# A two-layer vision tower: tokens of slots ahead of expert 0's rows, attention's end merged with the FFN's entry, and loads behind the K and Q casts

## The reference

```
h = patches(x) @ W_proj.T + b                     # 576 tokens (16 images x 36), 192 wide
h = h + attention(layernorm(h))                   # 12 heads of 64, softmax over the image's 36 tokens
h = h + ffn(layernorm(h))                         # BitLinear: rmsnorm, 8-bit activations, ternary weights
h = h + ttt_attention(layernorm(h))               # a state W1 per image and head, one gradient step
h = h + moe(layernorm(h))                         # 8 experts, the best 2 per token, capacity 180
```

## Time and profile before

| | |
|---|---|
| median of 3 runs | 268.79 us (268.14 to 273.12) |
| profiled execution, its own time | 268.12 us |
| its span, first to last instruction | 266.3 us |
| mean granted TensorE clock | 0.954 of 2.4 GHz |
| busy: PE, DVE, ACT, POOL | 229.8, 182.2, 160.1, 120.6 us |
| chain that ended last, by engine | PE 39%, DVE 26%, issue 11%, ACT 8%, POOL 8%, DMA 8% |

### The profile page before, as it was taken

The page is one execution under the profiler, slowest core; times in us unless marked ns, Lnnn a source line. Parts: engine busy times, 40 slices in busy tenths (PEclk is TensorE's granted clock), DMA queues, the critical chain, the costliest instruction groups (busy, mean ns, idle before and its releaser), DMA issues.

```text
span 266.3 us, 6234 instructions
## 1 busy us (share of the span) xinstructions
PE 229.8 (86%) x2368; PEld 176.0 (66%) x2368; DVE 182.2 (68%) x513; ACT 160.1 (60%) x302; POOL 120.6 (45%) x145
## 2 busy tenths in 40 slices
PE   8964899799489969988898999998999988999970
PEld 3741457587379956444496694975659778999960
DVE  1775367689998569779859879479875447455653
ACT  3623967878688970687589568384551384565300
POOL 9322199111323968564660005204304988845620
PEclk9999599999997988999999997999997999999996
DMA  6999785423290089990045005990660899842362
GB/s 192 296 275 187 116 197 138 99 61 69 61 219 16 2 148 203 205 202 11 0 39 72 0 2 50 137 138 4 68 132 28 135 158 176 110 77 29 33 149 72
DMA packets 25634, 28.66 MB, mean 108 GB/s; under 512 B 11624, under 2 KB 20897, under 8 KB 25509
## 3 DMA queue, kind: packets, MB, share of 16 engines
q0 software_dynamic: 7744, 15.43, 39.7%
q1 hardware_dynamic: 17861, 12.83, 17.2%
HBM read 36.74 MB, written 4.81 MB: 156 GB/s over the span
## 4 chain that ended last, share of the span: by engine, by line
PE 39%; DVE 26%; issue 11%; ACT 8%; POOL 8%; DMA 8%; DVEq 0%; SPq 0%; POOLq 0%; ACTq 0%
PE bank L656 6%; PE bank L568 5%; DMA arena<-x_scratch,arena 4%; PE bank L585 4%; PE bank L536 3%; DMA y_sum<-arena 3%; POOL arena L1922 3%; DVE st L968 3%; PE bank L523 2%; PE bank L746 2%; PE bank L904 2%; PE bank L915 2%; POOL y_sum L1913 2%; PE bank L723 2%; PE bank L764 2%
## 5 line engine op out<-in xcount | busy, mean ns | idle before, releaser
L656 PE MATMUL bank<-tri,idh 128*128 128x512 f16 x148 | 40.3, 395 | 0.0
L1913 POOL DMA_INDIRECT y_sum<-arena x12 | 18.0, 1500 | 9.3 <-DMA y_sum<-arena 4.9
L1922 POOL DMA_INDIRECT arena<-x_scratch,arena x14 | 13.9, 994 | 16.7 <-DVE arena L1448 12.8
L1841 POOL TENSOR_TENSOR arena<-arena,ri 128x432 f32<-128x432 f32 x8 | 7.3, 911 | 31.2 <-DVE ri L1089 31.2
L656 PEld LDWEIGHTS bank<-tri,idh 128*128 128x128 f16 x148 | 14.1, 101 | 10.9 <-issue 2.2
L1813 POOL TENSOR_TENSOR rs<-arg,mhalf 128x1 f32<-128x1 f32 (+1 forms) x20 | 11.9, 596 | 16.2 <-DVE arg L972 14.8
L585 PE MATMUL bank<-arena,arena_k 96*128 96x288 f16 (+2 forms) x144 | 18.5, 286 | 0.0
L1400 DVE TENSOR_TENSOR arena<-bank,arena 128x360 f32<-128x360 f32 x16 | 8.4, 532 | 13.6 <-PE bank L904 10.5
L585 PEld LDWEIGHTS bank<-arena,arena_k 96*128 96x128 f16 x144 | 13.8, 98 | 3.8 <-issue 0.3
L568 PE MATMUL bank<-arena_k,arena 96*128 96x384 f16 (+1 forms) x60 | 13.0, 389 | 3.6 <-issue 3.6
L447 POOL DMA_DIRECT2D arena_v<-in_w x4 | 3.2, 804 | 27.2 <-ACT arena_v L442 27.2
(11 more groups left out here) (292 smaller groups left out, 645.7 us busy)
## 6 DMA issues: line engine op xcount, KB each, us to landing
arena_k<-in_w POOLq DMA_DIRECT2D x8, 512.0 KB, 7.5
arena_v<-in_w POOLq DMA_DIRECT2D x8, 512.0 KB, 10.5
arena_v<-in_xT SPq DMA_DIRECT2D x6, 288.0 KB, 4.1
arena_v<-v_scratch SPq DMA_DIRECT2D x32, 54.0 KB
v_scratch<-arena SPq DMA_DIRECT2D x4, 384.0 KB, 3.7
arena_k<-in_w POOLq DMA_DIRECT2D x8, 192.0 KB, 9.0
arena_v<-in_w POOLq DMA_DIRECT2D x8, 192.0 KB, 11.4
arena_k<-in_wqkv POOLq DMA_DIRECT2D x4, 288.0 KB, 9.9
```

The source lines that it names most:

```text
L656: mm(bank[IDLE][:, :], idh[:, :], tri[:, 0:1].broadcast_to([128, 512]), start=True, stop=True)
L1913: nc.gpsimd.indirect_dma_start(y_sum[k][:, :], bass.IndirectOffsetOnAxis(ap=sum_at[:, k, e:e + 1], axis=0), ys[:, e, D * k:D * k + D], Non ...
L1922: nc.gpsimd.indirect_dma_start(zr[:, e - 1, XW * k:XW * k + XW], None, x_scr[:, :], bass.IndirectOffsetOnAxis(ap=tok_at[:, k, e:e + 1], ax ...
```

## The change

It has three parts. (1) SP waits for K's and Q's casting loads before it issues the rows, the FFN's weights and the tables, and ACT negates K's high half after the first two transposed tiles and not before them. (2) The loop over pairs ends at `PAIRS`, and what its last four steps held is written out in one order with the FFN's entry, on PE, ACT and DVE; the product `wz` of the second attention comes into it, POOL prepares the second attention's rows before its softmax products, and the FFN's own steps are reordered, with fewer `keep_awake`. (3) In the mixture of experts the tokens of all slots are marked and multiplied before expert 0's rows are selected; `xsp` holds the last 64 columns twice, so that the selection takes 20 matmuls and not 30; loads of the experts' low halves move by one in POOL's list. The diff, cut to its core:

```diff
+TAIL_ORDER = [("PT", 5), ("wo", 0), ("wz", 0), ("PV", 4), ("PV", 5), ("PT", 6), ("wo", 1), ("PT", 7), ("wo", 2),
+              ("PV", 6), ("PV", 7)]
-        xsp = carve(at, 2, NT, D, dt=F16)
+        xsp = carve(at, 2, NT, XW, dt=F16)
+        ohc = stage_a[:, 0:NT * CAP].bitcast(F16).rearrange("p (x i n) -> p x i n", x=2, i=NT)
...
-        FFN_ORDER = [("xiT", 0), ("xiT", 1), ("xiT", 2), ("gate", 0), ("gate", 1), ("xiT", 3), ("xiT", 4)] + [
-            ("gate", i) for i in range(2, NT)]
+        FFN_ORDER = [("xiT", 0), ("xiT", 1), ("xiT", 2), ("gate", 0), ("gate", 1), ("gate", 2), ("xiT", 3), ("xiT", 4),
+                     ("gate", 3), ("gate", 4)]
+        DOWN_ORDER = [("yiT", 0), ("down", 0), ("yiT", 1), ("yiT", 2), ("down", 1), ("yiT", 3), ("down", 2), ("yiT", 4),
+                      ("down", 3), ("down", 4)]
...
@@ SP
             load(wqkvraw[:, :, WV_AT:], "wv", d["wqkv"][:, :, WV_AT:])
+            sp.wait_ge(loaded("wk"), 16)
+            sp.wait_ge(loaded("wq"), 16)
             load(rows[:, 0:o], "rows", d["rows"][0:o].partition_broadcast(128))
...
@@ PE
+            stages = {"PT": transposes, "wo": output_projection, "wz": state_kernels, "PV": values}
+            for key, n in TAIL_ORDER:
+                stages[key](n)
             pe.wait_ge(free[IDLE], idle_from)
             pe.wait_ge(loaded("tri"), 16)
-            keep_awake(8)
+            keep_awake(3)
+            for i in range(3, NT):
+                output_projection(i)
...
-                if (key, i) == ("xiT", 2):
-                    keep_awake(3)
...
-            for i in range(NT):
-                r = rows_of(i)
-                if i == 0:
-                    keep_awake(10)
...
                 fills(ins, "yiT", i)
-                keep_awake(2)
...
                 fills(ins, "down", i)
-                keep_awake(5 if i == 3 else 2)
...
+            keep_awake(4)
+            for key, i in DOWN_ORDER:
+                (yi_transposed if key == "yiT" else ffn_down)(i)
+                if key == "yiT":
+                    keep_awake(2)
+            keep_awake(4)
             for i in range(NT):
                 x_transposed("x1T", 1, (i,))
-                keep_awake(2)
+                keep_awake(1)
...
             fills(ins, "pos")
-            keep_awake(8)
+            keep_awake(15)
...
-                for out0, out1, c0, o in ((0, 128, 0, 0), (0, DT, 128, CAP), (DT, 128, 128, CAP)):
+                for j in range(2):
                     for x in range(2):
...
-                            ins = mm(bk[out0:out1, o:o + CAP], xsp[0:r, x, i, c0:c0 + out1 - out0],
+                            ins = mm(bk[:, CAP * j:CAP * j + CAP], xsp[0:r, x, i, 128 * j:128 * j + 128],
                                      oh[0:r, i, :], start=i == 0 and x == 0, stop=i == NT - 1 and x == 1)
...
+            tokens_of_slots()
             rows_selected(0)
-            keep_awake(1)
-            tokens_of_slots()
-            keep_awake(1)
+            keep_awake(6)
             for s in range(E + 1):
                 if s < E:
                     up_gate(s)
-                if s == 0:
-                    slot_weights()
                 if s + 1 < E:
                     rows_transposed(s + 1)
...
                 if s == 0:
-                    keep_awake(6)
+                    slot_weights()
+                    keep_awake(2)
...
@@ DVE
+            softmax_sums(7)
+            residual(0)
+            centred(0)
+            bk = wait_full(dve, "wz")
+            dve.wait_ge(rows_made, 1)
+            frees(v.tensor_copy(wb[:, :, D:2 * D], bk[0:HF, 0:2 * D].rearrange("p (c n) -> p c n", c=2)), "wz")
+            read_low(3)
+            softmax_low(6)
+            read_low(4)
+            softmax_low(7)
+            read_low(5)
+            for i in range(1, 3):
+                residual(i)
+                centred(i)
+            read_low(6)
+            read_low(7)
+            quantised(0, 3)
+            for i in range(3, NT):
+                residual(i)
+                centred(i)
+            gated(0)
+            quantised(3, NT)
+            gated(1)
+            gated(2)
+            y_largest(0)
...
+            choices()
             onehots(0)
             x_low(range(2, NT))
-            choices()
-            z_low(0)
+            dve.wait_ge(xs_hi, NT + 1)
+            for r, c in ((128, slice(0, NT - 1)), (rows_of(NT - 1), slice(NT - 1, NT))):
+                ins = v.tensor_tensor(xsp[0:r, 1, c, D:], xs[0:r, c, 128:], xsp[0:r, 0, c, D:], ALU.subtract)
+            ins.then_inc(xs_done, 1)
             token_index()
             routing_weights()
+            z_low(0)
...
@@ ACT
-            act.wait_ge(loaded("wk"), 16)
-            a(wqkv[:, 1, :, 768:1536], wqkv[:, 0, :, 768:1536], ACT.Copy, scale=-1.0).then_inc(wqk_negated, 1)
             for i in range(NT):
                 r = rows_of(i)
+                if i == 2:
+                    act.wait_ge(loaded("wk"), 16)
+                    a(wqkv[:, 1, :, 768:1536], wqkv[:, 0, :, 768:1536], ACT.Copy, scale=-1.0).then_inc(wqk_negated, 1)
                 bk = wait_full(act, "xnT", i)
...
+            transposes_copied(5, 0)
+            act.wait_ge(wq_sum, 2)
+            a(wiq[:], stage13[:], ACT.Identity, bias=nmagic[0:HF, 0:1]).then_inc(wq_done, 1)
+            transposes_copied(5, 1)
+            read_high(3)
+            softmax_high(6)
+            read_high(4)
+            softmax_high(7)
+            a(w2q[:], stage2[:], ACT.Identity, bias=nmagic[:, 0:1]).then_inc(wq_done, 1)
+            read_high(5)
+            transposes_copied(6, 0)
+            transposes_copied(6, 1)
+            act.wait_ge(loaded("wa"), 16)
+            a(wa16[:, 0], wa[:, :, :], ACT.Copy).then_inc(tw_hi, 1)
+            transposes_copied(7, 0)
+            transposes_copied(7, 1)
+            read_high(6)
+            read_high(7)
+            wait_evac(act, "wz")
+            act.wait_ge(loaded("lrT"), 16)
+            act.wait_ge(rows_made, 1)
+            a(wb16[:, 0], wb[:, :, :], ACT.Copy).then_inc(tw_hi, 1)
             table(ACT.Silu)
...
+            for r, c in ((128, slice(0, NT - 1)), (rows_of(NT - 1), slice(NT - 1, NT))):
+                ins = a(xsp[0:r, 0, c, D:], xs[0:r, c, 128:], ACT.Copy)
+            ins.then_inc(xs_hi, 1)
...
-                if s == 1:
+                if s == 2:
                     negate_high(act, 7)
@@ POOL
+            for name in ("wvT", "wa", "tables"):
+                pool.wait_ge(loaded(name), 16 * len(TABLES) if name == "tables" else 16)
+            st_.do(g.tensor_tensor(rowb[:, 0:D], row("tb", TR), row("vb", TR), ALU.subtract))
...
+            pool.sem_inc(rows_made, 1)
             for p in range(PAIRS):
                 pool.wait_ge(rinved, p + 1)
...
-            for name in ("wvT", "wa", "tables"):
-                pool.wait_ge(loaded(name), 16 * len(TABLES) if name == "tables" else 16)
-            st_.do(g.tensor_tensor(rowb[:, 0:D], row("tb", TR), row("vb", TR), ALU.subtract))
...
-            pool.sem_inc(rows_made, 1)
             weight_low(0, wa, wa16)
...
             expert_low(pool, 3)
+            expert_low(pool, 4)
             for i in range(NT):
...
-            expert_low(pool, 4)
+            expert_low(pool, 5)
             pool.wait_ge(cleared, 48)
...
                 if e == 2:
+                    expert_low(pool, 6)
+                if e == 3:
                     expert_high(pool, E - 1)
-                if 2 <= e < 4:
-                    expert_low(pool, e + 3)
...
                 if e == 6:
+                    rows_added(1)
                     expert_low(pool, 7)
-                    rows_added(1)
```

417 lines of the change are left out of this document (218 added, 199 removed).

## The result

The changed kernel took **257.97 us** in the median of 4 runs (256.53 to 258.21), against 268.47 for the kernel before (4 runs, 267.57 to 273.12). The ratio is **0.9609, 95% interval 0.9557 to 0.9660**. The forecast of 256 with a range of 252 to 262.5 held. It was 2.0 too low.

What follows compares the result with a forecast made beforehand. No engine was taken to bound the whole; idle time on the chain sat at the start, attention's end with FFN's entry, and the experts. Gains 4.9 + 3.0 + 4.5 = 12.4 from 268.1 gave 255.7, said as 256, range 252 to 262.5.

Steps and rivals of the forecast that it cites:

- Front: Kernel's start: earlier V, then K and Q products starting at 35.5 instead of 40.4; 4.9 us gained, bounds 2.0 and 6.3.
- V's start at 24.4: Kernel's start: V's first matmul at about 24.4 instead of 27.41, 3.0 us gained.
- the landing of K's low half: Kernel's start: K's low weights land between 27.2 and 35.5 us; the late end was taken for K's and Q's start.
- Merge: Attention's end and FFN's entry: overlapping engine hops end the last normalised tile earlier; 3.0 us gained, bounds 0.5 and 5.5.
- The order of causes: FFN's entry: wa's cast, then POOL's loads and powers to 101.0, hold DVE; first FFN transpose at about 102.2, not 105.0.
- The clock rival: FFN to TTT: with fewer fillers PE's clock falls before the TTT products, costing 2.9 plus 1, time 260; chance 0.2.
- Experts: Mixture of experts: earlier gathers, no waits for rows, sums added sooner; 4.5 us gained, bounds 2 and 6.
- TensorE's part of the sum: Experts: 1.1 from expert 1's earlier start plus waits of 1.75 and 0.73 gone, less 0.5 for expert 7's negation: 3.1 us.
- Up and gate of expert 0: Experts: rows 1 to 1.4 later, but at kept clock they take 3.3 instead of 4.64 us and end where they did.
- the tail: Kernel's end: second sum added at about 255.5 instead of 260.51, giving 1.9 us where DVE waited for sums.
- signs of being wrong: Whole kernel: V's start moves but K's doesn't, low clock between 105 and 145, or scatters ending last as now.
- The slower rival: FFN through TTT: low clock stays; 25 us of such work eats the 12.4 gain, 275 needs 37; chance 0.04.

Runs made afterwards that it cites:

- experts_only: The kernel before with only the experts' part: tokens first, last 64 columns laid twice, loads, gathers and sums reordered; 272.82 us, ratio 1.0186.
- experts_again: The same kernel as experts_only, run a second time on another chip; 265.52 us, ratio 0.9914 to the kernel before.
- front_only: The kernel before with only K's negation moved inside ScalarE's row tiles and the sync queue's two waits; 262.12 us, ratio 0.9813.
- front_merge: The changed kernel without its experts' part, on the same chip as after_again; 260.0 us, ratio 0.9685 to the kernel before.
- after: The changed kernel in its first measurement and profile, against the kernel before; 257.97 us, ratio 0.9609.
- after_again: The changed kernel unaltered, measured again on the chip of front_merge, awake and awake_powers; 257.74 us, ratio 0.9532 to the kernel before.
- cols_once: The changed kernel with the last 64 columns laid once, so 30 selection products and not 20; 259.24 us, ratio 0.9703 to the kernel before.
- pool_order_old: The changed kernel with GpSimd's old order of expert loads and sums, and expert 7's negation one expert earlier; 259.28 us, ratio 0.9678 to the kernel before.
- act_order_only: The kernel before with only K's negation moved inside ScalarE's row tiles, without the sync queue's two waits; 264.42 us, ratio 0.9866.
- merge_only: The kernel before with only the merge of attention's end and the FFN's entry, new orders on four engines; 264.55 us, ratio 0.9799.
- awake: The changed kernel with filler matmuls in three TensorE holes: first scores, FFN, entry of the TTT's products; 254.46 us, ratio 0.9498 to the kernel before.
- awake_powers: As awake, with GpSimd's first three powers ahead of the loads of experts 4 to 6; 254.88 us, ratio 0.9466 to the kernel before.
- awake_all: As awake_powers, with two further holes filled in the pair loop; 255.54 us, ratio 0.9568 to the kernel before.

## Why the prediction was right, and where not

Several kernels share their code up to the mark, or from it on, so each stretch is measured more than once (us, one profile each):

```
to the mark     before, experts_only, experts_again            188.0 190.0 187.4
                front_only                                     181.1
                front_merge                                    180.1
                after, after_again, cols_once, pool_order_old  184.1 181.7 179.8 180.0
mark to end     before, front_only, act_order_only,
                merge_only, front_merge                        78.3 78.0 77.5 76.3 76.1
                after, after_again, experts_only,
                experts_again, awake, awake_powers, awake_all  72.2 73.3 76.8 76.3 72.7 75.1 76.0
```

front_merge belongs with the last group of the first stretch: up to the mark it is the changed kernel but for one load that GpSimd issues in an idle stretch (the same goes for pool_order_old). The same code differs by up to 4.3 to the mark and 4.6 behind it. The kernel before was read at its longest in the second stretch; the changed one at its longest in the first and its shortest in the second. By the means of the lines the split is 7.3 to the mark (188.4 and 181.1) and 2.6 behind it (77.2 and 74.6), where 3.9 and 6.1 were read and 7.9 and 4.5 predicted.

*Front: predicted 4.9; 6.3 at K's start, 6.9 at the mark in front_only, 6.4 by the medians, 5.0 by the ratios.* V's start at 24.4, the kept clock and V's end at 34.1 were right within 0.3. The mis-sized step is the landing of K's low half, which the sum took as late as 35.5, the casts' 13.5 us behind its issue. It was issued at 22.1 and landed at 31.5, Q's at 26.7 and 34.2, both before TensorE asked. First the casts, then the low halves, in the changed kernel:

```profile
DMA to landing us min/median/max: 6.7/7.0/7.3
```
```profile
DMA to landing us min/median/max: 7.5/8.4/9.3
```

The rule of the Trainium skill ("DMA: Bandwidth & Descriptors", Queues, rings and completion order), turns between the queues a packet at a time, had given the prediction an estimate of at most 10.4 us for K's low half, a landing at 32.4 and a gain of 6.3; the trace agrees with all three (9.3, 31.5, 6.3). Without the two waits K's and Q's products cost 1.3 more.

*Merge: predicted 3.0; on top of the front 2.7 by the medians, 3.4 by the ratios (0.0128 of 269), 1.0 at the mark.* The order of causes was right: the powers behind the wa cast and the expert loads, VectorE waiting 2.69. But TensorE's 2.88 ahead of tiles 3 and 4 was in no step, and in this profile 3.1 more went to the clock at the TTT's products (7.75 for 4.69). The clock rival had priced that at 2.9, with a chance of 0.2. It shows in the changed kernel's own profile. In front_merge and after_again, with the same code up to there, the clock is 1.00 at the TTT's entry (124 to 130 and 126 to 132), and they reach the mark 4.0 and 2.4 earlier. So it belongs to some runs of this code, and the removal of 28 fillers alone doesn't bring it there. At the FFN's hole the clock fell in all five profiles of front and merge that don't fill it.

*Experts: predicted 4.5; 2.3 by the medians, 4.1 by the ratios, 2.6 between the means of the two lines of the table (77.2 and 74.6).* TensorE's part of the sum, 3.1, was right: gathers 2 us earlier, 12.0 to 12.9 behind the mark for 14.1 to 14.2; no wait for gathered rows, where front_merge has 2.6; and expert 7's up and gate start on average 55.9 behind the mark for 58.8, 2.9 earlier, though single profiles lie from 54.0 to 59.0. Up and gate of expert 0 start 13.35 behind the mark before, were to start 1 to 1.4 later, and do so at 14.7 in after, awake and awake_powers; in the others the half level of the clock comes there and they start at 15.6 to 17.9.

The mis-sized step is the tail, from which 1.9 was to come. From the first combining product (253.88 and 245.90) to the end there are 12.4 us before and 10.4 after, so this pair of profiles shows it. The others don't: on average it is 10.6 in the first of the two lines "mark to end" (the old experts' part) and 10.9 in the second (the new). What the tail goes with is how far ahead of the first combining product GpSimd starts its last scatter-add: 0.5 in awake_powers (tail 13.2), 1.0 before (12.4), 2.6 in experts_only (12.8), 3.1 in six profiles (10.4 to 10.9), some 5 in the other five (8.9 to 9.4), of old and new order alike. Only in these last five does the second sum begin before TensorE's last product ends.

Sum: 6.4 + 2.7 + 2.3 = 11.4 by the medians of two chips, 10.5 in the first comparison, 12.4 predicted. The terms are known to 2 us at best, and none is off by clearly more. That 256 came within 2.0 is in part luck: by the medians the front was 1.5 too small and the experts 2.2 too large.

Two things that the prediction itself called signs of being wrong did show: a low clock between 105 and 145 (both low stretches there), and scatter-adds whose sum ends last as before. The time held all the same. Of the clock the total tells more than the places: from 24 to 240 us its mean is 0.95 before and 0.95 after, so the change moved the low stretches and left their sum as it was. The slower rival (37 us more of low clock) didn't come.

## What to carry to other kernels

Don't share out a gain between stages from one profile before and one after: here the same instructions up to one mark took 179.8 to 184.1 us. Take each stretch from several kernels that have the same code in it.

Don't credit a filler from one profile with it and one without: the same 36 products took 7.75 us in one profile of the changed kernel and 4.69 in another, and 4.69 with the filler. Look for a hole that has a low stretch in every profile, as the FFN's here. In a stage that another engine sets a filler gave nothing that could be told, and a low stretch came later, at the experts' entry.

A load that is deferred should be judged by what its absence speeds up: two waits on one queue gave 1.3 us because the casts landed 7 us sooner and with them Q's low half in time.

## What the runs showed of the hardware

The granted clock has only two levels in all these traces, 0.50 and 1.00 of 2.4 GHz, and one program falls to 1.2 GHz at different places from run to run: behind the hole of 1.02 at the TTT's entry the clock is 0.50 from 126 to 132 in after and 1.00 in after_again. Nor does every fall stand behind a hole. In the kernel before, TensorE was busy for 6.00 of 6.00 us from 150 to 156 at clock 1.00, then without a wait up to 160, and there it fell:

```profile
156.00:160.00 4.00, 4.00 (x42) 0.98 0.02 4
160.00:163.40 3.40, 3.40 (x10) 0.53 0.28 14
```

The Trainium skill ("TensorE: Matmul & The Clock Gate", HAM oscillation) puts a fall down to waits between bursts. The hole of 2.88 agrees with it. The fall at 160 doesn't, and at the hole of 1.85 one comes in experts_only and none in experts_again, the same program; there the measurements decide.

A VectorE operation on three columns took 0.27 us, and the same on two columns 1.27, when it started beside a GpSimd product of 1.27:

```profile
96.75 0.27 DVE L1155 TENSOR_SCALAR am<-am 128x3 f32<-128x3 f32 x1
...
102.61 1.27 POOL L1967 TENSOR_TENSOR arena<-arena,rows 128x512 f32<-128x512 f32 x1 [0.71 <-DVE arena L1171]
102.63 1.27 DVE L1155 TENSOR_SCALAR am<-am 128x2 f32<-128x2 f32 x1
```

In after_again the same operation took 1.26 at the same place, beside the same product of 1.27. The Trainium skill ("SBUF — State Buffer", SBUF: two separate sides) says that GpSimd and a VectorE operation in a 2-port mode, or with two inputs from SBUF, exclude each other at a shared port pair for a whole instruction. These rows agree; in which mode this operation ran no run shows. The 1.0 lies on the chain to the FFN's fourth transpose.
